# Two recurrences on one core: a lookup pair is moved from the large cell of the second recurrence to its small cell

## The chip, the cores and the metric

The kernel runs on one core of one Trainium2 chip. The metric is the device time of one execution in microseconds (us), shown as the median of three runs. Engines are named as in the profile: PE is TensorE's matmuls, PEld its weight loads, DVE is VectorE, ACT is ScalarE, POOL is GpSimd, SP is SyncE, which issues the DMAs.

## The reference

```python
B, LS, LN = 512, 64, 32
FM = [0, 0, 1, 1, 2, 2, 3, 3, 4, 5, 5]
...
        def step(carry, xt):
            h, c = carry
            g = xt @ Wx + h @ Wh + b
            i, f, gg, o = jnp.split(g, 4, axis=-1)
            c = jax.nn.sigmoid(f) * c + jax.nn.sigmoid(i) * jnp.tanh(gg)
            h = jax.nn.sigmoid(o) * jnp.tanh(c)
            return ((h, c), None)
...
m_from = lstm_last(base_emb[from_seq], seq_Wx, seq_Wh, seq_b)
m_to = lstm_last(base_emb[to_seq], seq_Wx, seq_Wh, seq_b)
...
        x = jnp.concatenate([ne[nums], fe[fr]], axis=-1)
        return lstm_last(x, Wx, Wh, b)
nwf = jax.vmap(enc)(nwf_num_emb[fm], nwf_freq_emb[fm], nwf_Wx[fm], nwf_Wh[fm], nwf_b[fm], nwf_numbers, nwf_freqs)
...
return jax.nn.relu(feats @ reduce_W + reduce_b)
```

The inputs have 2048 rows. There are two kinds of recurrence (LSTM). The first, `seq`, takes 64 steps with a state of 64 values over two token sequences that share their weights. The second, `nwf`, takes 32 steps with a state of 8 values for 11 features that use 6 sets of weights. Each of its steps looks up a number and a frequency in tables of 1000 rows. The last states and some single lookups go through one final matrix product.

## The kernel before

**Cells.** A step of a recurrence for one half of its data is a cell. `CELLS` sets one order of all cells, and every engine follows it. In a round r from 1 to 31 the order is: A and B, the two halves of `seq` step 2r; C, the large half of `nwf` step r-1 (features 0 to 7, 1024 columns); D and E, the two halves of `seq` step 2r+1; F, the small half of `nwf` step r-1 (features 8 to 10, 384 columns). The letters are used throughout. A round has six cells; round 0 has only its four `seq` cells, and a last round has only C and F.

**A cell** computes four gates on PE (`gate`, L515). Gates 0, 1 and 3 go through two PSUM buffers, `ab0` and `ab1`, used in turn; the forget gate has its own, `f_ps`. ACT applies the functions (`activate`, L555, L562, L564; `activate_f`) and releases the `ab` buffer. POOL multiplies gates 0 and 1 (`input_product`, `ig`, L585), DVE scales the old cell state (`scale_c`, L593) and adds (`add_c`, L598, at the start of the next cell), ACT takes the tanh (L555), POOL makes the new state (`new_h`, L612).

**Lookups** for `nwf` run beside the cells. The index of a table row is split into a low digit (0 to 127) and a high digit (0 to 7). Eleven pairs of lookups (0 to 10) belong to each round. For one pair, SP loads the low digits on all 128 partitions and the high digits (L416, L421); DVE compares (`compare_pair`, `hot`, L428); PE multiplies the one-hot matrix with the tables into `e_ps` (`look_up`, 24 matmuls, L438); DVE keeps the part that the high digit asks for (`keep_wanted`, `kept`, L450). There is one `e_ps`, so a look_up waits for the keep_wanted of the pair before it. A compare is made two pairs ahead of its look_up, into two `hot` buffers. Once both types of a feature set are kept, PE reduces them to that set's input (`set_input`, L465) in an `ab` buffer, and ACT copies it out (`store_x`, L478). Sets 0 to 3 and 5 take two pairs each, set 4 takes pair 8 alone.

**Where they stand.** `PAIRS_AT` gives each cell its pairs; `SETS_AT` gives the cell after a set's last pair that set's input. In a `seq` cell PE's order is gate 0, first look_up, set inputs, gate 1, second look_up, lookup of a later `seq` token (L401), forget gate, gate 3. In an `nwf` cell the set inputs and the first look_up stand ahead of gate 0:

```python
                    if CELLS[n][0] == "seq":
                        gate(pe, n, 0)
                        for p in pairs[:1]:
                            look_up(pe, p)
                        sum_sets(pe, n)
                    else:
                        sum_sets(pe, n)
                        for p in pairs[:1]:
                            look_up(pe, p)
                        gate(pe, n, 0)
                    gate(pe, n, 1)
                    for p in pairs[1:]:
                        look_up(pe, p)
```

The order of use of `ab0` and `ab1` is the list `USES`; `begin_use` makes PE wait until ACT has released the use two before. DVE's order in a cell is add_c of the cell before, first keep_wanted, compare of a `seq` token (L390), in F of rounds 1 to 29 the splitting of a later round's indices into digits (`make_digits`, L314 to L339), two compares, second keep_wanted, scale_c. POOL waits ahead of `input_product` until the compares of its cell are done. SP issues the loads of a pair four pairs ahead, each after the compare that frees its buffer.

Of the kernel before, what the change touches and what calls it, by code (L numbers as in the profile page):

```python
# [71 lines left out]
SETS_AT = [[] for _ in CELLS]  # L72
for _r in range(NWF_T):
    _j = NPAIRS * _r
    _share = [3, 3, 3, 2] if _r == 0 else [2, 2, 2, 2, 2, 1]
    _first = NUMBER["seq", 2 * _r, 0]
    for _k, _n in enumerate(_share):
        PAIRS_AT[_first + _k] = list(range(_j, _j + _n))
        _j += _n
        SETS_AT[_first + _k + 1] += [(_r, m) for m in range(NSETS)  # L80
                                     if _j - _n <= NPAIRS * _r + SET_LAST[m] < _j]
# [827 lines left out]
```

## Time and profile before

| | |
|---|---|
| median of 3 runs | 1803.08 us (1800.8 to 1803.32) |
| the profiled execution | 1799.57 us, its span 1797.7 us |
| mean granted clock of TensorE | 0.987 |
| PE busy | 93% of the span |
| DVE, ACT busy | 81% each |
| POOL busy | 53% |
| chain that ended last | PE 64%, ACT 18%, POOL 7%, issue 6%, DMA 1% |
| read from HBM | 474.17 MB, with the writes 267 GB/s |

The span runs from the first to the last instruction. The shares are means over a ramp of some 120 us, 31 rounds that look alike and a short end. "Idle" in a row is the time in which the row's engine had nothing to run just before it, with the instruction that ended the wait. A wait is told by its idle time or, since matmuls overlap, by the distance from one start to the next.

### The profile page before, as it was taken

To read this page: it belongs to the slowest core of one execution; us is meant where nothing else is said; L and a number is where in the kernel's file an instruction comes from. 1 tells how busy PE (TensorE), PEld (TensorE's weight loads), DVE (VectorE), ACT (ScalarE), POOL (GpSimd) and SP (SyncE) were. 2 spreads that over 40 slices of the span, in tenths; PEclk is the share of its full clock that TensorE was granted. 3 is DMA by queue.
4 is the path that set the end of the run, shared out by engine and by line. 5 is a ranking of instruction groups with operands and counts; after the bars stand their busy time and mean duration, and the time that the engine had idled before them with its cause. 6 is when DMAs were issued, how large, how long until landed. Compare 5 with 4: busy or idle time off the path is not lost.

```text
span 1797.7 us, 59515 instructions
## 1 busy us (share of the span) xinstructions
PE 1680.6 (93%) x24900; PEld 765.0 (43%) x24900; DVE 1462.9 (81%) x1443; ACT 1464.5 (81%) x2531; POOL 944.8 (53%) x478
## 2 busy tenths in 40 slices
PE   2789999999999999999999999999999999999995
PEld 0234444444444444444444444444444444444444
DVE  6768888888888888988888888888888888888771
ACT  1468888888888888888888888888888888888883
POOL 5346666666666666444444444444554444444552
PEclk9899999999999999999999999999999999999997
DMA  6868898999988988889898888989888888888832
GB/s 224 299 223 261 281 290 285 275 289 277 293 279 284 286 284 285 276 270 298 277 284 289 275 277 278 290 277 285 280 286 279 282 272 296 283 277 282 282 119 49
DMA packets 153476, 484.37 MB, mean 269 GB/s; under 512 B 39240, under 2 KB 95096, under 8 KB 108024
## 3 DMA queue, kind: packets, MB, share of 16 engines
q1 hardware_dynamic: 149532, 479.52, 82.5%
q8 instruction: 198, 3.24, 0.7%
q0 software_dynamic: 2560, 0.15, 0.5%
q10 hardware_dynamic: 1116, 0.88, 0.1%
q14 instruction: 70, 0.57, 0.1%
HBM read 474.17 MB, written 6.09 MB: 267 GB/s over the span
## 4 chain that ended last, share of the span: by engine, by line
PE 64%; ACT 18%; POOL 7%; issue 6%; DMA 1%; SPq 0%; DVE 0%; ACTq 0%; POOLq 0%
PE ab L515 28%; PE e_ps L438 15%; PE f_ps L515 10%; ACT gate L555 10%; PE ab L465 7%; POOL nwf_h L612 4%; ACT tanh_c L555 4%; POOL ig L585 4%; PE ab L401 3%; ACT seq_x L408 2%; ACT f_ps L564 1%; ACT gate L564 1%; ACT nwf_x L478 1%; DMA last_h<-nwf_h 0%; PE e_ps L828 0%
## 5 line engine op out<-in xcount | busy, mean ns | idle before, releaser
L585 POOL TENSOR_TENSOR ig<-gate 128x1024 f32<-128x1024 f32 x192 | 411.1, 2141 | 810.1 <-ACT seq_x L408 404.2
L428 DVE TENSOR_SCALAR hot<-low,cst 128x4096 bf16<-128x4096 bf16 x352 | 453.4, 1288 | 152.8 <-PE e_ps L438 149.4
L438 PE MATMUL e_ps<-hot,tab 128*32 128x512 bf16 x8448 | 527.2, 384 | 15.9 <-DVE kept L450 15.9
L450 DVE SCALAR_TENSOR_TENSOR kept<-high,cst,e_ps 128x1024 f32<-128x1024 uint8 x352 | 448.8, 1275 | 32.9 <-PE e_ps L438 22.1
L515 PE MATMUL ab<-seq_h,seq_wh 64*64 64x512 f32 x3072 | 411.0, 593 | 0.0
L438 PEld LDWEIGHTS e_ps<-hot,tab 128*32 128x32 bf16 x8448 | 204.3, 97 | 399.0 <-issue 228.9
L612 POOL TENSOR_TENSOR seq_h<-gate,tanh_c 128x1024 f32<-128x1024 f32 x128 | 303.9, 2374 | 1.4 <-ACT tanh_c L555 1.4
L562 ACT ACTIVATE gate<-ab 128x1024 f32<-128x1024 f32 x256 | 263.2, 1028 | 18.2 <-PE ab L515 15.0
L555 ACT ACTIVATE tanh_c<-seq_c 64x512 f32<-64x512 f32 (+1 forms) x384 | 241.9, 630 | 25.3 <-POOL nwf_h L612 22.2
L555 ACT ACTIVATE gate<-ab 64x512 f32<-64x512 f32 (+1 forms) x384 | 228.3, 595 | 11.5
L564 ACT ACTIVATE gate<-ab,nwf_bias 128x256 f32<-128x256 f32 (+1 forms) x384 | 147.4, 456 | 104.0 <-PE ab L515 99.9
L465 PE MATMUL ab<-kept,cst 128*32 128x256 f32 (+1 forms) x3072 | 189.5, 365 | 28.7 <-ACT gate L555 28.7
L515 PE MATMUL ab<-nwf_x,nwf_w 64*64 64x256 f32 (+1 forms) x2304 | 201.6, 366 | 7.2 <-ACT gate L555 5.5
L515 PE MATMUL ab<-nwf_h,nwf_w 64*64 64x256 f32 (+1 forms) x2304 | 204.9, 361 | 0.0
L408 ACT CAST seq_x<-ab 128x1024 bf16<-128x1024 f32 x128 | 129.6, 1013 | 69.7 <-PE ab L401 65.5
L593 DVE TENSOR_TENSOR f_ps<-seq_c,f_ps 128x1024 f32<-128x1024 f32 x128 | 157.3, 1229 | 28.8 <-ACT f_ps L562 16.7
L515 PE MATMUL ab<-seq_x,seq_wx 64*64 64x512 bf16 x1536 | 165.2, 385 | 10.0 <-issue 7.2
L598 DVE TENSOR_TENSOR seq_c<-ig,f_ps 128x1024 f32<-128x1024 f32 x128 | 156.3, 1221 | 8.3 <-POOL ig L585 3.3
L515 PEld LDWEIGHTS ab<-seq_h,seq_wh 64*64 64x64 f32 x3072 | 118.5, 133 | 89.4 <-issue 60.1
L562 ACT ACTIVATE f_ps<-f_ps 128x1024 f32<-128x1024 f32 x128 | 129.0, 1008 | 27.7 <-PE f_ps L515 27.7
L465 PEld LDWEIGHTS ab<-kept,cst 128*32 128x32 f32 x3072 | 88.3, 109 | 148.1 <-issue 59.0
L555 ACT ACTIVATE gate<-ab,nwf_bias 64x256 f32<-64x256 f32 (+2 forms) x288 | 125.4, 447 | 9.2 <-PE ab L515 5.9
(67 smaller groups left out, 1608.5 us busy)
## 6 DMA issues: line engine op xcount, KB each, us to landing
low<-low_digits SPq DMA_DIRECT2D x352, 1024.0 KB, 8.0
tok<-seq_tokens SPq DMA_DIRECT2D x128, 384.0 KB, 4.9
high<-high_digits SPq DMA_DIRECT2D x1408, 32.0 KB
raw<-in_indices SPq DMA_DIRECT2D x32, 176.0 KB
low_digits<-low_of SPq DMA_DIRECT2D x32, 88.0 KB, 3.0
high_digits<-high_of SPq DMA_DIRECT2D x32, 44.0 KB, 3.6
gate<-in_tokens SPq DMA_DIRECT2D x1, 1024.0 KB, 5.7
low<-last_h SPq DMA_DIRECT2D x11, 64.0 KB
```

Of the source, the lines that this page charges most:

```text
L408: nc.scalar.copy(seq_x[:, s % X_RING, :, :], ab[USE["sx", s] % 2][:, :, :]).then_inc(ab_done, 1)
L428: nc.vector.tensor_scalar(hot[:, p % HOT_RING, :, :, :].rearrange("p g u c -> p (g u c)"), low[:, p % LOW_RING, :, :].rearrange("p u c -> ...
L438: last = nc.tensor.matmul(e_ps[32 * g:32 * g + 32, i, :], tab[:, part, 2 * m + ty, :], hot[:, p % HOT_RING, g, i, :], start=(part == 0), s ...
L450: nc.vector.scalar_tensor_tensor(out=kept[:, p % KEPT_RING, :, :].rearrange("p u c -> p (u c)"), in0=high[:, p % HIGH_RING, :, :].rearrang ...
L465: last = nc.tensor.matmul(to[32 * q:32 * q + 32, 0, 0:n], cst[:, C_RED + 32 * ty:C_RED + 32 * ty + 32], kept[:, (NPAIRS * r + p) % KEPT_RI ...
L515: last = nc.tensor.matmul(flat(bank)[to:to + 64, cols], lhs(rows, half, block), rhs(rows, block, a, b), start=start, stop=stop)
L555: last = nc.scalar.activation(to[rows, a:a + c], of[there, a:a + c], function, bias=0.0 if bias is None else bias[there, :])
L562: return nc.scalar.activation(to, of, GATES[g][1])
L564: last = nc.scalar.activation(to[:, a:a + c], of[:, a:a + c], GATES[g][1], bias=bias)
L585: nc.gpsimd.tensor_tensor(ig[:, cols], gates[0][:, n % 2, cols], gates[1][:, n % 2, cols], ALU.mult).then_inc(ig_ready, 1)
L593: nc.vector.tensor_tensor(f, c_of(n), f, ALU.mult).then_inc(c_scaled, 1)
L612: nc.gpsimd.tensor_tensor(h_of(n), gates[3][:, n % 2, cols], tanh_c[:, cols], ALU.mult).then_inc(h_ready, 1)
```

## The change

One line of the table of pairs: in rounds 1 to 31 the large cell C gets one pair in place of two and the small cell F two in place of one. Cells D and E keep two pairs each, but of numbers one lower: D gets 5 and 6 (6 and 7 before), E gets 7 and 8 (8 and 9), F gets 9 and 10 (10). The places of the set inputs follow from this. Set 2 moves from D to E, set 3 from E to F, where it now stands ahead of set 4. Set 1 in C and set 5 in A stay.

```diff
-    _share = [3, 3, 3, 2] if _r == 0 else [2, 2, 2, 2, 2, 1]
+    _share = [3, 3, 3, 2] if _r == 0 else [2, 2, 1, 2, 2, 2]
```

On PE in C, before, from gate 1's last matmuls to the forget gate (`e_ps` is the second look_up):

```order
L515 MATMUL ab1<-nwf_h0,nwf_w 64x256 x4
L438 MATMUL e_ps<-hot,tab 32x512 x24
L515 MATMUL f_ps<-nwf_x,nwf_w 64x256 x4
L515 MATMUL f_ps<-nwf_h0,nwf_w 64x256 x4
L515 MATMUL f_ps<-nwf_x,nwf_w 64x256 x4
```

Behind it on PE in D, before, from gate 0 to the token lookup (`kept` is the input of set 2):

```order
L515 MATMUL ab1<-seq_x,seq_wx 64x512 x4
L515 MATMUL ab1<-seq_h,seq_wh 64x512 x4
L438 MATMUL e_ps<-hot,tab 32x512 x24
L465 MATMUL ab0<-kept,cst 32x256 x8
L515 MATMUL ab1<-seq_x,seq_wx 64x512 x4
L515 MATMUL ab1<-seq_h,seq_wh 64x512 x4
L438 MATMUL e_ps<-hot,tab 32x512 x24
L401 MATMUL ab0<-seq_hot,seq_tab 32x512 x8
```

The same piece of D with the change:

```order
L515 MATMUL ab1<-seq_x,seq_wx 64x512 x4
L515 MATMUL ab1<-seq_h,seq_wh 64x512 x4
L438 MATMUL e_ps<-hot,tab 32x512 x24
L515 MATMUL ab0<-seq_x,seq_wx 64x512 x4
L515 MATMUL ab0<-seq_h,seq_wh 64x512 x4
L438 MATMUL e_ps<-hot,tab 32x512 x24
L401 MATMUL ab1<-seq_hot,seq_tab 32x512 x8
```

The second look_up of C is gone, D has no set input, and D's gate 1 takes `ab0`, which C's gate 3 used last.

On PE from E's gate 3 into F, before (the `32x128` row is set 4's input):

```order
L515 MATMUL ab0<-seq_h,seq_wh 64x512 x4
L465 MATMUL ab1<-kept,cst 32x128 x8
L438 MATMUL e_ps<-hot,tab 32x512 x24
L515 MATMUL ab0<-nwf_x,nwf_w 64x256 x2
L515 MATMUL ab0<-nwf_x,nwf_w 64x128 x2
```

And with the change:

```order
L515 MATMUL ab1<-seq_h,seq_wh 64x512 x4
L465 MATMUL ab0<-kept,cst 32x256 x8
L465 MATMUL ab1<-kept,cst 32x128 x8
L438 MATMUL e_ps<-hot,tab 32x512 x24
L515 MATMUL ab0<-nwf_x,nwf_w 64x256 x2
L515 MATMUL ab0<-nwf_x,nwf_w 64x128 x2
```

Two set inputs stand in a row, and the second takes `ab1`, the buffer of E's gate 3. A second look_up stands later in F, between gate 1 and the forget gate.

On DVE in F and into A, before, from the splitting of digits to A's token compare:

```order
L339 CAST high_of<-wrap 128x352
L428 TENSOR_SCALAR hot<-low,cst 128x4096
L593 TENSOR_TENSOR f_ps<-nwf_c,f_ps 128x384
L598 TENSOR_TENSOR nwf_c<-ig,f_ps 128x384
L450 SCALAR_TENSOR_TENSOR kept<-high,cst,e_ps 128x1024
L390 TENSOR_SCALAR seq_hot<-tok,cst 96x2048
```

And with the change:

```order
L339 CAST high_of<-wrap 128x352
L428 TENSOR_SCALAR hot<-low,cst 128x4096 x2
L450 SCALAR_TENSOR_TENSOR kept<-high,cst,e_ps 128x1024
L593 TENSOR_TENSOR f_ps<-nwf_c,f_ps 128x384
L598 TENSOR_TENSOR nwf_c<-ig,f_ps 128x384
L450 SCALAR_TENSOR_TENSOR kept<-high,cst,e_ps 128x1024
L390 TENSOR_SCALAR seq_hot<-tok,cst 96x2048
```

A second compare and a second keep_wanted now stand between the digits and the state of F. On SP the token loads of D and E move ahead of one pair's loads each; POOL's order is the same.

## Rows read from the trace of the kernel before

**Rows 1.** The page, part 1: busy time of each engine, share of the span.
```profile
PE 1680.6 (93%) x24900; PEld 765.0 (43%) x24900; DVE 1462.9 (81%) x1443; ACT 1464.5 (81%) x2531; POOL 944.8 (53%) x478
```
**Rows 2.** Timeline of DVE, add_c of F in two rounds: start us, us, instruction.
```profile
1171.15 0.55 DVE L598 TENSOR_TENSOR nwf_c<-ig,f_ps 128x384 f32<-128x384 f32 x1
...
1224.04 0.56 DVE L598 TENSOR_TENSOR nwf_c<-ig,f_ps 128x384 f32<-128x384 f32 x1
```
**Rows 3.** Timeline of PE, C into D (last bracket: idle before, and releaser).
```profile
1192.76 1.48 PE L438 MATMUL e_ps<-hot,tab 128*32 128x512 bf16 x24
1194.17 0.66 PE L515 MATMUL f_ps<-nwf_x,nwf_w 64*64 64x256 f32 x8
...
1198.86 1.48 PE L438 MATMUL e_ps<-hot,tab 128*32 128x512 bf16 x24
1200.83 1.07 PE L465 MATMUL ab<-kept,cst 128*32 128x256 f32 x16 [0.50 <-ACT gate L555]
1201.83 0.41 PE L515 MATMUL ab<-seq_x,seq_wx 64*64 64x512 bf16 x4
...
1203.03 1.48 PE L438 MATMUL e_ps<-hot,tab 128*32 128x512 bf16 x24
1204.34 0.61 PE L401 MATMUL ab<-seq_hot,seq_tab 96*32 96x512 bf16 x8
```
**Rows 4.** Timeline of ACT in C: gate 1, forget gate, gate 3.
```profile
1192.90 1.57 ACT L564 ACTIVATE gate<-ab,nwf_bias 128x256 f32<-128x256 f32 x4 [0.16 <-PE ab L515]
...
1196.19 1.54 ACT L564 ACTIVATE f_ps<-f_ps,nwf_bias 128x256 f32<-128x256 f32 x4
1197.92 2.77 ACT L555 ACTIVATE gate<-ab,nwf_bias 128x256 f32<-128x256 f32 x6 [0.18 <-PE ab L515]
```
**Rows 5.** Timeline of PE, E through F into A.
```profile
1211.69 1.48 PE L438 MATMUL e_ps<-hot,tab 128*32 128x512 bf16 x24
1213.31 0.61 PE L401 MATMUL ab<-seq_hot,seq_tab 96*32 96x512 bf16 x8
...
1214.95 0.39 PE L515 MATMUL ab<-seq_x,seq_wx 64*64 64x512 bf16 x4
...
1216.12 0.65 PE L465 MATMUL ab<-kept,cst 128*32 128x128 f32 x16
1216.59 1.48 PE L438 MATMUL e_ps<-hot,tab 128*32 128x512 bf16 x24
1218.22 0.65 PE L515 MATMUL ab<-nwf_x,nwf_w 64*64 64x256 f32 x8 [0.16 <-ACT gate L555]
...
1222.90 1.48 PE L438 MATMUL e_ps<-hot,tab 128*32 128x512 bf16 x24
1224.75 1.07 PE L465 MATMUL ab<-kept,cst 128*32 128x256 f32 x16 [0.37 <-ACT gate L555]
```
**Rows 6.** Timeline of ACT, gate 3 of E.
```profile
1216.27 1.81 ACT L555 ACTIVATE gate<-ab 128x512 f32<-128x512 f32 x3
```
**Rows 7.** Timeline of DVE in F: keep_wanted, later the compare.
```profile
1218.64 1.27 DVE L450 SCALAR_TENSOR_TENSOR kept<-high,cst,e_ps 128x1024 f32<-128x1024 uint8 x1
...
1221.57 1.28 DVE L428 TENSOR_SCALAR hot<-low,cst 128x4096 bf16<-128x4096 bf16 x1
```
**Rows 8.** Timeline of DVE in A and B: the token compare in each.
```profile
1172.81 1.12 DVE L390 TENSOR_SCALAR seq_hot<-tok,cst 96x2048 bf16<-96x2048 bf16 x1
...
1182.03 0.75 DVE L390 TENSOR_SCALAR seq_hot<-tok,cst 96x2048 bf16<-96x2048 bf16 x1
```
**Rows 9.** Timeline of PE, two long waits outside the rounds.
```profile
64.10 2.33 PE L438 MATMUL e_ps<-hot,tab 128*32 128x512 bf16 x20 [2.75 <-DVE kept L450]
...
1753.73 1.07 PE L465 MATMUL ab<-kept,cst 128*32 128x256 f32 x16 [2.27 <-ACT gate L555]
```
**Rows 10.** Stretches: us; busy (count) of PE, PEld, DVE, ACT, POOL; PEclk; DMA share; GB/s.
```profile
63.70:67.10 3.40, 3.00 (x32) 1.27 (x32) 0.40 (x2) 0.00 (x0) 3.40 (x2) 0.50 0.77 274
1750.00:1756.00 6.00, 3.73 (x57) 2.25 (x54) 1.12 (x2) 4.47 (x10) 3.35 (x2) 1.00 0.02 4
```

## The prediction, made before the changed kernel was run

> **What bounds the kernel now.** The page's busy times come first: PE is busy for 93% of the span, DVE and ACT for 81% each [rows 1]. Such shares don't tell what a moved step costs, so the next view is the timeline of one round. The same add of F stands at 1171.15 and at 1224.04, so a round takes 52.89 us [rows 2], and 31 rounds with lookups make some 1640 of the 1797.7 us. In a round PE hardly rests. The reader is to see where its few waits stand and who ends them. In D, from the first look_up to set 2's input is 1.97 us, where a look_up that is followed without a wait has a slot of 1.31 (1203.03 to 1204.34); ACT's gate 3 of C ends that wait [rows 3]. In E the token lookup comes 1.62 after the look_up, 0.31 late. In A set 5's input comes 1.85 after the look_up, 0.54 late. In F gate 0 comes exactly 3.27 after gate 3 of E began (1214.95 to 1218.22) and is again released by ACT [rows 5]. So PE's work and the release of the two `ab` buffers by ACT bound the round together. ACT is the tight one in C: its gates there follow each other with idle times of 0.16 and 0.18 us [rows 4].
>
> **The change, part by part.** The number of matmuls, compares, keeps, copies and DMAs is the same. What counts is where PE's pieces meet a wait. Times below are those of the shown round, carried on as if the change began in its C.
>
> *C and D.* PE loses the second look_up of C, a slot of 1.41 us (1192.76 to 1194.17), and in D set 2's input, 1.00 us (1200.83 to 1201.83), with its wait of 0.66 [rows 3]. If all of that counted, D's gate 1 would come 3.07 us earlier. But D's gate 1 now needs the buffer of C's gate 3, which ACT releases. ACT's forget gate in C ends at 1197.73 and its gate 3 takes 2.77 [rows 4]; with PE earlier it loses only its idle 0.18 and ends at 1200.51. A release is followed by PE 0.14 us later (1200.69 to 1200.83), so D's gate 1 starts at 1200.65 instead of 1201.83: **1.18 us** gained. PE has then stood since its look_up, which now begins at 1197.45 and runs 1.48: a new wait of about 1.7 us (1.9 against its slot). DVE's and POOL's part of C gets shorter too, but the cell state of C needs ACT's forget gate, which hardly moves, so nothing is gained there.
>
> *E.* D still ends on the same pieces, and the 0.31 us that the token lookup waits in E falls away, because the set copy it needs comes as early as the rest; about 0.1 comes back where gate 1 waits for ACT's gate 0. Gate 3 of E begins 1.18 + 0.31 - 0.1 = **1.4 us** earlier.
>
> *F, first half.* Set 3's input stands 1.17 us after gate 3 of E, as set 4's did. Set 4's input now needs the buffer of E's gate 3. Before, it was F's gate 0 that needed it, and set 4's input and the look_up ran inside that wait: ACT's gate 3 takes 1.81 and ends 3.13 after PE's gate 3 began [rows 5, 6]. So set 4's input comes 3.27 after gate 3 of E, and behind it, in PE's order, stand the look_up and gate 0. Its own slot is 0.47 (1216.12 to 1216.59), the look_up's 1.41, so gate 0 comes 5.15 after gate 3 of E instead of 3.27: **1.88 us** lost. Set 3's input, 1.07 us long, lies inside the wait and leaves PE idle for about 1.0.
>
> *F, second half, and A.* The new look_up between gate 1 and the forget gate costs its slot of **1.41**. By PE alone A's look_up would then stand 7.95 (1214.95 to 1222.90) + 1.88 + 1.41 = 11.24 after gate 3 of E. It waits for the keep of pair 10, which DVE now makes at the end of F. The keep of pair 9 starts when its look_up is done, 3.27 + 0.47 + 1.48 = 5.22 after gate 3 of E; from a keep to the first compare is 2.93 with the digits between them [rows 7]; each compare moves DVE on by 1.2 and the keep ends 1.27 after it starts. That is 5.22 + 2.93 + 1.2 + 1.2 + 1.27 = 11.82, and A's look_up starts about 0.1 later, at 11.9: **0.6 us** of new wait. A's old wait of 0.54 for ACT falls away, since ACT has had the time.
>
> *Sum.* -1.4 + 1.88 + 1.41 + 0.6 - 0.54 = **+1.95, say 2.0 us a round**. In the rest of A and in B everything is shifted alike, so the round repeats with this. Twenty-nine rounds have digits in F; without them the last two have no wait for the keep of pair 10 and, at the end, some of the cost falls into the wait of 2.27 us in front of the last C [rows 9]. 29 x 2.0 + about 2 = 60 us.
>
> *What I cost at nothing.* The token loads on SP that move ahead of one pair's loads, and those loads: a pair is loaded four ahead, which is more than a cell, and the longer round gives them more time. If they came late, a compare would wait for a DMA. POOL's product in F now waits for the second compare of F; what it feeds, the cell state and tanh of F, is wanted on PE only a round later. Cover gone, it would delay ACT in A. POOL and DVE together are the unknown: the token compare takes 1.12 us in A, with POOL at work, and 0.75 in B [rows 8]. In the new stretch of F the digits and compares should find POOL at rest. The bounds for that stretch are no wait at all (0.6 less) and 0.37 more, the difference of those two rows, for each of F's two compares (0.75 more). I take neither: the row of B, without POOL, is the nearer one, and the durations in the sum are of that kind.
>
> A pause of PE of this length is where its clock comes in. In the ramp a wait of 2.75 us ended at 64.10, and the granted clock of the 3.4 us from 63.70 was 0.50, which is 1.2 of 2.4 GHz; near the end PE waited 2.27 us up to 1753.73, and the clock stayed at 1.00 [rows 9, 10]. The new waits of 1.7, 1.0 and 0.6 are all shorter than that, so the sum has no term for it. The Trainium skill ("TensorE: Matmul & The Clock Gate", Part 1: The HAM clock gate) says that the throttled rate is the default state and that activity releases it; this speaks against any change that makes PE pause. The row at 64.10 agrees with it, and no row here shows a fall after a pause as short as the new ones. By the rows the sum is +60; by the rule, were these pauses enough, it is that of the second rival below.
>
> The sum is made against the profiled execution, 1799.57 us, and gives 1859.6. The median of the runs is 3.5 us above that execution, so for the median I say **1863 us**, 3.3% slower.
>
> **The rivals.**
>
> 1. *DVE is not late* (chance 0.10). The keep of pair 10 comes in time and 0.6 a round falls away: 1.4 x 31 = 43, 1846 us. For it: it rests on five DVE steps in a row, each rounded. Against: there is no wait among them that could shrink.
>
> 2. *The clock falls* in D's new wait (0.05). A fall costs half of 3.4 us, 1.7 a round: 3.7 x 31 = 115, 1918 us. For it: the clock did fall after a pause of 2.75. Against it: it did not after one of 2.27, and the forecast's longest is 1.7 [rows 9, 10].
>
> 3. *Faster: ACT follows PE* (0.03). If ACT in C and E is late only because PE feeds it late, then with PE ahead both releases come earlier, and D's 1.9 and set 4's 1.2 beyond its slot in F vanish: 2.0 - 3.1 = -1.1 a round, -34, 1769 us. It turns from slower to faster once ACT's gate 3 of C ends about 1.2 us before 1200.51. Against it: in C there are only 0.16 and 0.18 of idle time between ACT's gates [rows 4], so it can't move by 1.2.
>
> 4. *Nothing moves* (0.02): the 1.41 of C and the 1.41 of F cancel, and the other waits too; 1803 us. That the change doesn't do what it says can be left out: the order of instructions shows pair 5 behind D's gate 0 and two look_ups in F.
>
> **How the numbers follow.** The forecast has 0.75, rival 1 0.10, the others 0.10 together; 0.05 is left for a slower outcome of another size. The range takes in rival 1 and the bounds of the DVE stretch: at the low end 0.6 a round less and another 0.2 of rounding, 1.2 x 31 = 37, 1840; at the high end 2.75 x 31 = 85, 1888. It leaves out rivals 2 to 4 and the rest of the unlikely. Measurements of this kernel can tell about 0.2%, 3.6 us, from no change. Faster by more 0.03, within it 0.02, slower by more 0.95.
>
> **What would show it.** In the profile after: rounds of 54.9 us; in D, PE's gate 1 about 3.2 us after the look_up, released by ACT's gate 3 (L555), a wait of some 1.7; in F, two L465 in a row with about 1 us of idle time between them, released by the same line; in A, the look_up waiting some 0.6 for DVE's keep (L450); the wait of A's set input gone; the clock at 1.00 through all rounds. Wrong would be a gate 1 of D that starts right after its look_up, a second L465 in F without a wait, or a granted clock below 1 between 120 and 1750 us.

## The result, and the profile after

| | before | after |
|---|---|---|
| median (runs) | 1803.2 us (1800.8 to 1805.72, 4) | 1863.38 us (1861.24 to 1864.23, 4) |
| ratio, 95% interval | | 1.0332 [1.0314, 1.035] |
| span of the profiled execution | 1797.7 us | 1862.4 us (execution 1864.23) |
| round without a stall of PE | 52.89 us | 55.12 us |

The kernel became 60 us slower. The changed kernel's page gives the busy times, the granted clock by slices, and the chain that ended last:

```profile
PE 1680.3 (90%) x24900; PEld 759.7 (41%) x24900; DVE 1446.3 (78%) x1443; ACT 1459.9 (78%) x2531; POOL 929.1 (50%) x478
...
PEclk9899999999999999999999999999999999999997
...
PE 49%; DVE 17%; ACT 13%; POOL 8%; issue 7%; DMA 1%; DVEq 0%; SPq 0%; POOLq 0%; ACTq 0%
```

PE is busy for the same 1680 us as in [rows 1], in a span that is 65 us longer: the change added no work, it added waits. In the chain PE's share fell from 64% to 49%, and DVE's, 17%, is new. The same add of F as in [rows 2], timeline of DVE, in two rounds of the changed kernel:

```profile
1213.20 0.55 DVE L598 TENSOR_TENSOR nwf_c<-ig,f_ps 128x384 f32<-128x384 f32 x1
...
1268.33 0.55 DVE L598 TENSOR_TENSOR nwf_c<-ig,f_ps 128x384 f32<-128x384 f32 x1
```

A round takes 55.13 us here, 2.24 more than before. PE's waits, from the list of waits (us in total, times, longest):

```profile
PE ab L515 <- ACT gate L555: 50.0, 31, 1.8
PE ab L465 <- ACT gate L555: 32.7, 32, 1.0
PE e_ps L438 <- DVE kept L450: 31.6, 30, 8.9
```

There are three per round: D's gate 1, the second set input of F, the first look_up of A. The sums hold the ramp and the end too: the wait of 8.9 us in the third row lies in the ramp. The three stand in the timeline of PE as follows. C into D (answers to [rows 3]):

```profile
1229.99 1.48 PE L438 MATMUL e_ps<-hot,tab 128*32 128x512 bf16 x24
1231.40 0.66 PE L515 MATMUL ab<-nwf_x,nwf_w 64*64 64x256 f32 x8
...
1239.54 1.48 PE L438 MATMUL e_ps<-hot,tab 128*32 128x512 bf16 x24
1242.77 0.41 PE L515 MATMUL ab<-seq_x,seq_wx 64*64 64x512 bf16 x4 [1.75 <-ACT gate L555]
```

E through F into A (answers to [rows 5]):

```profile
1252.63 1.48 PE L438 MATMUL e_ps<-hot,tab 128*32 128x512 bf16 x24
1254.26 0.62 PE L401 MATMUL ab<-seq_hot,seq_tab 96*32 96x512 bf16 x8 [0.15 <-ACT nwf_x L478]
...
1255.91 0.39 PE L515 MATMUL ab<-seq_x,seq_wx 64*64 64x512 bf16 x4
...
1257.08 1.07 PE L465 MATMUL ab<-kept,cst 128*32 128x256 f32 x16
1259.18 0.65 PE L465 MATMUL ab<-kept,cst 128*32 128x128 f32 x16 [1.03 <-ACT gate L555]
1259.61 1.50 PE L438 MATMUL e_ps<-hot,tab 128*32 128x512 bf16 x24
1261.05 0.65 PE L515 MATMUL ab<-nwf_x,nwf_w 64*64 64x256 f32 x8
...
1262.92 1.48 PE L438 MATMUL e_ps<-hot,tab 128*32 128x512 bf16 x24
...
1267.97 1.48 PE L438 MATMUL e_ps<-hot,tab 128*32 128x512 bf16 x24 [0.62 <-DVE kept L450]
1269.26 1.05 PE L465 MATMUL ab<-kept,cst 128*32 128x256 f32 x16
```

Behind each wait stands its releaser. Timeline of ACT: forget gate and gate 3 of C ([rows 4]), tanh of D's state and a set copy in E, gate 3 of E ([rows 6]):

```profile
1238.43 1.50 ACT L564 ACTIVATE f_ps<-f_ps,nwf_bias 128x256 f32<-128x256 f32 x4
1239.95 2.77 ACT L555 ACTIVATE gate<-ab,nwf_bias 128x256 f32<-128x256 f32 x6
...
1251.80 1.92 ACT L555 ACTIVATE tanh_c<-seq_c 128x512 f32<-128x512 f32 x3 [0.59 <-POOL nwf_h L612]
1253.75 0.37 ACT L478 COPY nwf_x<-ab 128x256 f32<-128x256 f32 x1
...
1257.23 1.81 ACT L555 ACTIVATE gate<-ab 128x512 f32<-128x512 f32 x3
```

Timeline of DVE in F ([rows 7]): keep of pair 9, the two compares behind the digits, keep of pair 10.

```profile
1261.22 1.28 DVE L450 SCALAR_TENSOR_TENSOR kept<-high,cst,e_ps 128x1024 f32<-128x1024 uint8 x1 [1.53 <-PE e_ps L438]
...
1264.15 2.48 DVE L428 TENSOR_SCALAR hot<-low,cst 128x4096 bf16<-128x4096 bf16 x2
1266.55 1.28 DVE L450 SCALAR_TENSOR_TENSOR kept<-high,cst,e_ps 128x1024 f32<-128x1024 uint8 x1
```

ACT's gate 3 of C ends at 1242.72, and PE's gate 1 of D follows at 1242.77. ACT's gate 3 of E ends at 1259.04, and set 4's input follows at 1259.18. DVE's keep of pair 10 ends at 1267.83, and A's look_up follows at 1267.97.

### The profile page after: what moved, and what is told of

Its sections match the earlier page's. It is cut to its first block, busy times and chain, and to the rows that moved or that the text cites. A ratio compares the mean times of both kernels' runs of the same rounds, so it can differ in the third digit from the quotient of the medians.

```text
span 1862.4 us, 59515 instructions
## 1 busy us (share of the span) xinstructions
PE 1680.3 (90%) x24900; PEld 759.7 (41%) x24900; DVE 1446.3 (78%) x1443; ACT 1459.9 (78%) x2531; POOL 929.1 (50%) x478
## 3 DMA queue, kind: packets, MB, share of 16 engines
q8 instruction: 198, 3.24, 0.7%
## 4 chain that ended last, share of the span: by engine, by line
PE 49%; DVE 17%; ACT 13%; POOL 8%; issue 7%; DMA 1%; DVEq 0%; SPq 0%; POOLq 0%; ACTq 0%
PE ab L515 19%; PE e_ps L438 15%; PE f_ps L515 6%; DVE hot L428 6%; PE ab L465 6%; DVE kept L450 5%; ACT tanh_c L555 4%; POOL nwf_h L612 4%; POOL ig L585 4%; ACT gate L555 3%; ACT f_ps L564 3%; PE ab L401 3%; ACT gate L564 2%; DVE f_ps L593 2%; DVE seq_hot L390 1%
## 5 line engine op out<-in xcount | busy, mean ns | idle before, releaser
L438 PE MATMUL e_ps<-hot,tab 128*32 128x512 bf16 x8448 | 528.2, 384 | 31.7 <-DVE kept L450 31.6
L450 DVE SCALAR_TENSOR_TENSOR kept<-high,cst,e_ps 128x1024 f32<-128x1024 uint8 x352 | 449.1, 1276 | 94.4 <-PE e_ps L438 81.8
L428 DVE TENSOR_SCALAR hot<-low,cst 128x4096 bf16<-128x4096 bf16 x352 | 448.7, 1282 | 37.4 <-PE e_ps L438 31.6
L438 PEld LDWEIGHTS e_ps<-hot,tab 128*32 128x32 bf16 x8448 | 210.8, 97 | 410.1 <-issue 260.1
L555 ACT ACTIVATE tanh_c<-seq_c 64x512 f32<-64x512 f32 (+1 forms) x384 | 241.8, 630 | 22.7 <-POOL nwf_h L612 19.6
L564 ACT ACTIVATE gate<-ab,nwf_bias 128x256 f32<-128x256 f32 (+1 forms) x384 | 147.4, 456 | 137.7 <-PE ab L515 132.3
L555 ACT ACTIVATE gate<-ab 64x512 f32<-64x512 f32 (+1 forms) x384 | 228.4, 595 | 9.5
L465 PE MATMUL ab<-kept,cst 128*32 128x256 f32 (+1 forms) x3072 | 188.8, 364 | 32.7 <-ACT gate L555 32.7
L593 DVE TENSOR_TENSOR f_ps<-nwf_c,f_ps 128x1024 f32<-128x1024 f32 x64 | 57.1, 892 | 196.8 <-ACT f_ps L564 196.8
L465 PEld LDWEIGHTS ab<-kept,cst 128*32 128x32 f32 x3072 | 88.7, 109 | 145.4 <-issue 49.9
```

The source lines that it names most:

```text
L428: nc.vector.tensor_scalar(hot[:, p % HOT_RING, :, :, :].rearrange("p g u c -> p (g u c)"), low[:, p % LOW_RING, :, :].rearrange("p u c -> ...
L438: last = nc.tensor.matmul(e_ps[32 * g:32 * g + 32, i, :], tab[:, part, 2 * m + ty, :], hot[:, p % HOT_RING, g, i, :], start=(part == 0), s ...
L450: nc.vector.scalar_tensor_tensor(out=kept[:, p % KEPT_RING, :, :].rearrange("p u c -> p (u c)"), in0=high[:, p % HIGH_RING, :, :].rearrang ...
L465: last = nc.tensor.matmul(to[32 * q:32 * q + 32, 0, 0:n], cst[:, C_RED + 32 * ty:C_RED + 32 * ty + 32], kept[:, (NPAIRS * r + p) % KEPT_RI ...
L555: last = nc.scalar.activation(to[rows, a:a + c], of[there, a:a + c], function, bias=0.0 if bias is None else bias[there, :])
L564: last = nc.scalar.activation(to[:, a:a + c], of[:, a:a + c], GATES[g][1], bias=bias)
```

## The experiments

Times are medians; a ratio is to the kernel before, measured on the same chip (medians there 1801.5 to 1802.7 us). "Round" is a round without a stall of PE; the last part tells what those stalls are. Where a kernel has one line more, L438, L450, L465 and L555 appear as L439, L451, L466 and L556.

### The first half of F: a look_up between the two set inputs

Changed kernel, order of PE in C and F:

```diff
-                        sum_sets(pe, n)
+                        for r, m in SETS_AT[n][:1]:
+                            set_input(pe, r, m)
                         for p in pairs[:1]:
                             look_up(pe, p)
+                        for r, m in SETS_AT[n][1:]:
+                            set_input(pe, r, m)
```

> The changed kernel, with F's first look_up between its two set inputs instead of behind both. My theory: set 4's input waits 1.0 us for the buffer of E's gate 3, and the look_up behind it could have run in that time. F's gate 0 then comes 3.96 us after gate 3 of E instead of 5.14; DVE's keep of pair 9 starts about 1.5 earlier, so A's look_up comes at 10.5 instead of 12.06 after gate 3 of E: 1.56 x 31 = 48 us less, 1815. Rival, the loss in F is the moved PE work itself and no wait: within 5 us of 1863.

Measured: 1814.62 us, ratio 1.007 [1.0054, 1.0087]; round 53.50. PE's timeline, set 4's input in F and A's look_up:

```profile
1227.63 0.62 PE L465 MATMUL ab<-kept,cst 128*32 128x128 f32 x16
...
1234.70 1.48 PE L438 MATMUL e_ps<-hot,tab 128*32 128x512 bf16 x24 [0.23 <-DVE kept L450]
```

The look_up runs inside the time in which ACT finishes gate 3 of E, and the wait of 1.03 is gone. Keep 9 starts earlier with its look_up, so A's wait shrinks from 0.62 to 0.23 as well. No work was removed, and 49 of the 60 us came back. So most of the net loss is an order in which two set inputs stand next to each other and the second needs a buffer that is not yet free.

### The second half of F: who sets the start of A

Changed kernel, the digits made in C:

```diff
-ROUND_AT = {(2 if _r == 2 else NUMBER["nwf", _r - 3, 1]): _r
+ROUND_AT = {(2 if _r == 2 else NUMBER["nwf", _r - 3, 0]): _r
...
```

> The changed kernel, with the splitting of digits moved from F to C of the same round, where DVE stands idle for 5.9 us. My theory: in F the digits lie on DVE's chain to the keep of pair 10, for which A's look_up waits 0.62 us a round. Without them in F the keep comes 1.7 us earlier and PE alone sets that look_up: 0.6 x 29 = 18 us less, 1845. Rival, DVE is not what A waits for: 1863, unchanged.

Measured: 1846.44 us, ratio 1.0247 [1.0228, 1.0266]; round 54.42, that is 0.70 less. A's look_up has no wait any more, while D's 1.74 and F's 1.03 stay:

```profile
1193.34 0.64 PE L465 MATMUL ab<-kept,cst 128*32 128x128 f32 x16 [1.03 <-ACT gate L555]
...
1201.44 1.48 PE L438 MATMUL e_ps<-hot,tab 128*32 128x512 bf16 x24
```

Changed kernel, F's second look_up (pair 10) cut to 8 of its 24 matmuls:

```diff
+                parts = 1 if p % NPAIRS == 10 and p >= NPAIRS else 3
-                for part in range(3):
+                for part in range(parts):
```

> The changed kernel, with F's second look_up (pair 10) doing 8 of its 24 matmuls, the second and third part of the table values left out for that pair. 0.85 us of PE is taken from F each round. My theory: A's look_up waits for DVE's keep of pair 10, whose chain starts at the look_up of pair 9 and does not wait for that of pair 10, so the wait only gets longer: 1863, unchanged within 3 us. Rival, the second look_up costs its PE time: 0.85 x 31 = 26 us less, 1837.

Measured: 1862.53 us, ratio 1.0341 [1.032, 1.0361]; round 55.13. What PE saves in F it waits in A:

```profile
1212.47 1.48 PE L439 MATMUL e_ps<-hot,tab 128*32 128x512 bf16 x24 [1.49 <-DVE kept L451]
```

The wait grew from 0.62 to 1.49, by the 0.87 that the look_up lost. In the changed kernel the end of F belongs to DVE's row of keep, digits, two compares and keep, and no longer to PE.

### C and D: what a look_up in C is worth

Kernel before, C's second look_up (pair 5) cut in the same way to 8 of 24 matmuls:

```diff
+                parts = 1 if p % NPAIRS == 5 and p >= NPAIRS else 3
-                for part in range(3):
+                for part in range(parts):
```

> The kernel before, with C's second look_up (pair 5) doing 8 of its 24 matmuls: the second and third part of the table values are left out for that pair. 0.85 us of PE is taken from C each round. My theory: behind C, D waits for ACT's gate 3 of C, which can come only 0.2 us earlier, so the gain is 0.2 x 31 = 6 us, 1797. Rival, PE bounds C and its work counts in full: 0.85 x 31 = 26 us, 1777.

Measured: 1792.02 us, ratio 0.9948 [0.993, 0.9966]. The cut took 27 us of PE's work (31 rounds of 0.87) and the time fell by 10. Over the rounds, the median from C's second look_up to D's first fell from 6.10 to 5.23, all of the 0.87; from there to D's second look_up it rose from 4.17 to 4.81, so D gave 0.64 back. Set 2's input in D, which waited 0.50 in [rows 3]:

```profile
1033.96 1.07 PE L466 MATMUL ab<-kept,cst 128*32 128x256 f32 x16 [1.13 <-ACT gate L556]
```

The rest, 0.23 a round, is 7 of the 10 us. The forecast of 1797 was 5 us too high, and the rival's 1777 is further off: three quarters of a look_up's work in C go into the wait for ACT.

The next edit takes the same place from the other side. ACT's gate 3 of C is written as whole-width instructions instead of two halves that change places. It was tried once in the changed kernel, once in the kernel before (`whole` marks the gates that keep their old form; C's gate 3 is the one that gets the new one):

```diff
-            last = at_h(to, of, pieces(n, g), GATES[g][1]) if g == 3 else in_place(to, of, n, g)
+            whole = g == 3 and CELLS[n][0] == "seq" or g == 3 and CELLS[n][2] == 1
+            last = at_h(to, of, pieces(n, g), GATES[g][1]) if whole else in_place(to, of, n, g)
```

> The changed kernel, with ACT's gate 3 of C done as whole-width instructions like gates 0 and 1 (the exchange of the two halves of the second feature block is left out), 1.57 us instead of 2.77. D's gate 1 is then released 1.2 us earlier. My theory: behind it D's second look_up needs the keep of pair 5, which DVE makes after the add of C, and that comes no earlier; so only 0.3 of the 1.2 counts: 9 us less, 1854. Rival, ACT's gate 3 alone sets D: 1.2 x 31 = 37 us less, 1826.

Measured: 1856.21 us, ratio 1.0292 [1.0272, 1.0313]; round 54.94. PE in D:

```profile
1236.75 0.41 PE L515 MATMUL ab<-seq_x,seq_wx 64*64 64x512 bf16 x4 [0.55 <-ACT gate L564]
...
1238.96 1.48 PE L438 MATMUL e_ps<-hot,tab 128*32 128x512 bf16 x24 [0.94 <-DVE kept L450]
```

The wait for ACT fell from 1.75 to 0.55, and 0.94 of the 1.20 came back two rows later as a wait for DVE, whose keep stands behind the new cell state of C. So ACT's gate 3 held D up, and DVE's keep is the next to do so, only 0.2 us earlier.

> The kernel before with ScalarE's gate 3 of C as whole-width instructions (the exchange of halves is left out, so part of the new state of C is not computed as in the reference). In the kernel before, set 2's input in D waits for this gate, with PE idle for 0.66 us. In the changed kernel the same edit took 7 us (from 1863.4 to 1856.2), 0.25 us a round. Theory, D's release is the only thing that the gate 3 of C holds up: if the edit shortens ScalarE's gate 3 by as much as it did there, the release comes 0.2 to 0.7 us earlier, 6 to 20 us less, 1782 to 1796. Rival, ScalarE is late in C before gate 3 and the gate's form does not matter: 1800 to 1803.

Measured: 1778.38 us, ratio 0.9867 [0.9852, 0.9882]; round 52.19, which is 0.70 less. D runs without any wait:

```profile
1186.36 1.48 PE L438 MATMUL e_ps<-hot,tab 128*32 128x512 bf16 x24
1187.67 1.04 PE L465 MATMUL ab<-kept,cst 128*32 128x256 f32 x16
```

The gain of 23 us is beyond the forecast's end of 20: the wait of 0.66 went whole in all 31 rounds (31 x 0.70 = 22). The rival falls. Here no wait for DVE takes its place.

### Put together

The changed kernel with both orders, digits in C and look_up between the set inputs:

> The changed kernel with both edits: the look_up between F's set inputs, and the digits in C. With the look_up moved, A still waits 0.22 us for DVE's keep; without the digits in F that goes too. My theory: 0.25 to 0.45 us a round less than with the look_up alone, 1802 to 1807, so that the whole loss in F is undone and only the gain of C and D set against the moved look_up is left: about the kernel before. Rival, another wait takes their place: 1815 or more.

Measured: 1810.83 us, ratio 1.0042 [1.0027, 1.0056]: a miss. The round is 53.19, 0.3 below that of the look_up between the set inputs, as expected. But PE stood more often with no releaser that the profile names: over 29 rounds the mean is 53.60 with the look_up alone, 0.10 above a round without a stall, and 53.52 with both, 0.33 above. The "issue" row of PE's waits, first with the look_up between the set inputs alone, then with both:

```profile
PE ab L515 <- issue: 11.4, 7, 3.6
```

```profile
PE ab L515 <- issue: 21.3, 18, 3.6
```

Not all of these are stalls. Three in each row (8.9 us) lie in the ramp and the end, and one of the 7 (1.9 us) and five of the 18 (6.2 us) are D's gate 1, which starts 0.05 us after ACT's gate has ended, as in the rows with a named releaser. What is left went from 3 (0.6 us) to 10 (6.3 us).

Both kernels still lose 1.74 in D. ACT in C stands in order gate 0, gate 1, tanh of B's state, forget gate, gate 3, and before gate 0 it idles (1.99 us in the changed kernel, `ACT L564 gate`, while PE works on C's first matmuls). So ACT's tanh of the cell before was moved ahead of gate 0 in C and F, with a second `tanh_c` buffer. First in the kernel before:

```diff
+                        tanh_of(act, n - 1)
                     activate(act, n, 0)
...
                     activate(act, n, 1)
-                    if not is_seq:
-                        tanh_of(act, n - 1)
```

> The kernel before with the same edit of ACT's tanh and its second buffer alone. My theory: C with two look_ups is bound by PE at gate 3, so D gains nothing; E's 0.3 and A's 0.5 us of wait go: 0.8 x 31 = 25 us less, 1778. It tells how much of the edit's worth needs the pairs moved. Rival, the edit is worth the same in both: 1750.

Measured: 1790.36 us, ratio 0.994 [0.992, 0.996]; round 52.66, only 0.23 less, and 12 us in all where 25 were forecast. PE in D and F:

```profile
1194.81 1.07 PE L465 MATMUL ab<-kept,cst 128*32 128x256 f32 x16 [0.49 <-ACT gate L555]
...
1215.14 0.65 PE L515 MATMUL ab<-nwf_x,nwf_w 64*64 64x256 f32 x8 [0.46 <-ACT gate L564]
```

D's wait stays at 0.49: in C ACT now waits 1.73 us for PE's forget gate, which stands behind the second look_up, so here ACT follows PE. E's and A's waits did go: the token lookup of E comes 1.30 after the look_up (1.62 before), set 5's input in A 1.30 after its look_up (1.85 before). But F's gate 3 got a wait of 0.46 for ACT's gate 0 of F, which now stands behind the tanh, and the way from F's gate 0 to A's look_up grew from 4.68 to 5.35. Then in the changed kernel with both orders:

> The third edit on top of both: in C and F ACT takes the tanh of the cell before ahead of gate 0 instead of behind gate 1, with a second tanh buffer so that it need not wait for POOL. ACT idles 2 us ahead of gate 0 in both cells. My theory: C's forget gate and gate 3 on ACT come 1.4 us earlier, the add of C with them, so D's wait of 1.75 shrinks to 0.35; E's token lookup no longer waits 0.3 for POOL. 1.7 x 31 = 53 us less than both edits, 1752, faster than the kernel before by 2.8%. Rival, PE or DVE takes the wait's place in D: no better than 1790.

Measured: 1771.08 us, ratio 0.9833 [0.9808, 0.9857]. The round is 51.52, 1.67 below that with both orders (1.7 forecast), and D's wait fell from 1.74 to 0.40. The time is 19 us above the forecast: the mean of its 29 rounds is 52.14, 0.62 above a round without a stall. The last kernel has the same, with the digits back in F:

> The changed kernel with F's first look_up put between its two set inputs (as in lookup_between, 1814.6 us) and, in the large and small cells, ScalarE's tanh of the previous cell put ahead of gate 0 (as in both_tanh, 1771.1 us), but with pair digits made in F as the change has them. It tells apart where the irregular rounds of both_tanh come from, in which PE is late in C and F without a wait that the profile shows. Forecast for an undisturbed round: both_tanh's 51.5 us, or up to 0.25 more, since the keep of pair 10 gets the wait of A's look_up back (0.22 in lookup_between). Theory 1, the digits in C bring the irregular rounds: here they are as few as in lookup_between (mean round 0.1 over an undisturbed one), mean 51.6 to 51.9, about 1755 to 1763 us. Theory 2, they come wherever PE runs without a wait, digits or not: mean round 0.6 over an undisturbed one as in both_tanh, 52.1 to 52.4, about 1771 to 1778 us.

Measured: 1763.43 us, ratio 0.9789 [0.9776, 0.9803], faster than both kernels. The round is 51.83 and the mean of 29 is 52.02. A's look_up and D's gate 1:

```profile
1200.35 1.48 PE L438 MATMUL e_ps<-hot,tab 128*32 128x512 bf16 x24 [0.24 <-DVE kept L450]
...
1228.94 0.41 PE L515 MATMUL ab<-seq_x,seq_wx 64*64 64x512 bf16 x4 [0.40 <-ACT gate L555]
```

Its round is 0.31 longer than with the digits in C, and yet it is some 8 us faster; the excess of the mean over a round without a stall is 0.19 us instead of 0.62. Theory 1 (the digits in C bring the stalls) had the excess at 0.1 and 1755 to 1763 us, theory 2 at 0.6 and 1771 to 1778: neither holds it, the first is nearer. The excess is that of one profiled execution of each kernel, and those two have nearly the same span (1765.8 us here, 1764.6 with the digits in C), so it carries less than the medians. Why the digits on DVE should matter to PE's stalls no run shows.

## Why the prediction was right

The forecast was 1863 us and the median came at 1863.38. Term by term, from the distances on PE in the shown round (before to after):

| stretch | predicted | measured |
|---|---|---|
| C's first set input to D's gate 1 | -1.18 | 14.98 to 13.66, -1.32 |
| D's gate 1 to E's gate 3 | -0.21 | 13.12 to 13.14, +0.02 |
| E's gate 3 to F's gate 0 | +1.88 | 3.27 to 5.14, +1.87 |
| F's gate 0 to A's look_up | +1.41 + 0.6 | 4.68 to 6.92, +2.24 |
| A's look_up to A's gate 1 | -0.54 | 2.85 to 2.27, -0.58 |
| sum | +1.95 | +2.24 (with 0.01 elsewhere) |

*D* was right in its mechanism: two slots of PE's work, 2.41 us, left the path, and of the 3.07 of work and wait 1.32 came back as time. PE's new wait of 1.75 (predicted 1.7) ends with ACT's gate 3 of C. The whole-width gate 3 moved it in both kernels; the two cuts show that a look_up's work counts for a quarter in C of the kernel before and for nothing in F of the changed one, where another engine sets the next release. The 0.14 that the term fell short is ACT's gate 3, 0.23 earlier instead of 0.18, and PE's start 0.05 after it (1242.72 to 1242.77) instead of 0.14.

*E* is the step that failed. I wrote that the 0.31 us of the token lookup would fall away "because the set copy it needs comes as early as the rest". It came 1.63 after the look_up, as before (1.62 in [rows 5]). The copy did come as early as the rest, and just that keeps the wait: from C's set input to the copy is 1.30 less than before, and to D's gate 1 1.32 less. To take the wait away, the copy had to gain 0.31 more than PE. What ties the two together, before, in timelines of DVE, POOL and ACT (second compare of D, new state of C, the copy):

```profile
1204.64 1.29 DVE L428 TENSOR_SCALAR hot<-low,cst 128x4096 bf16<-128x4096 bf16 x1 [1.06 <-PE e_ps L438]
...
1208.38 2.38 POOL L612 TENSOR_TENSOR nwf_h<-gate,tanh_c 128x1024 f32<-128x1024 f32 x1
...
1212.79 0.37 ACT L478 COPY nwf_x<-ab 128x256 f32<-128x256 f32 x1
```

And with the change, in timelines of DVE and POOL (both compares of D, product of D, new state of C):

```profile
1244.22 2.64 DVE L428 TENSOR_SCALAR hot<-low,cst 128x4096 bf16<-128x4096 bf16 x2
...
1247.00 2.37 POOL L585 TENSOR_TENSOR ig<-gate 128x1024 f32<-128x1024 f32 x1 [5.46 <-DVE hot L428]
1249.33 2.38 POOL L612 TENSOR_TENSOR nwf_h<-gate,tanh_c 128x1024 f32<-128x1024 f32 x1
```

The copy at 1253.75 stands on ACT behind the tanh of D, and that waits for POOL's new state of C. On POOL that state stands behind the product of D, which waits for DVE's second compare of D, and this compare needs the `hot` buffer that PE's second look_up of D frees. That look_up ends at 1204.51 before and at 1245.45 with the change, and the copy starts 8.28 and 8.30 later. So the copy follows PE's own work in D and moves with it. The tanh moved in the kernel before shows the link: with the second `tanh_c` buffer the tanh of D no longer waits for POOL, and E's wait is gone (1.30 from look_up to token lookup).

*F's first half* was right to 0.01 us, the wait being 1.03 (predicted about 1.0). Putting the look_up between the two set inputs took away that wait.

*F's second half and A*: the mechanism was right, the sum 0.23 short. From E's gate 3 to A's look_up it took 12.06 instead of 11.9: keep 9 started 5.31 after that gate (5.22 predicted), the keep to the first compare took 2.93 and the two compares 2.40 as predicted, and PE followed the keep after 0.14 instead of 0.1. Also 11.9 less 11.24 is 0.66, which the text rounded to 0.6. The row with POOL at rest was the right one to take for the compares: 2.40 for two. The loads, costed at nothing, cost nothing more: compares wait 3.3 us in all for low digits, in the kernel before as in the changed one.

The total was closer than its parts, and that is luck. 0.29 a round too little is 8 us over 29 rounds. Against it stand the rounds with a stall of PE: over 29 rounds the mean is 53.06 in the kernel before, 0.17 above a round without one, and 55.16 in the changed kernel, 0.03 above. So the mean round grew by 2.10 us, 61 in 29 rounds, where I had 58; the sum has no term for stalls. The last rounds and the end took 3.4 us more, where I had about 2. The profiled span grew by 64.7, and the medians, 1803.2 and 1863.38, lie 60 apart.

*The rivals.* DVE was late by 0.62 (rival 1 falls; the digits in C and the cut in F show the wait each in its way). The clock did not fall (rival 2). The stretches hold the pauses of D and F (columns as in [rows 10]):

```profile
1241.00:1243.00 2.00, 0.25 (x8) 0.17 (x8) 1.97 (x3) 1.94 (x5) 0.54 (x1) 1.00 0.04 16
...
1256.00:1260.00 4.00, 2.97 (x56) 1.37 (x52) 3.16 (x3) 3.28 (x6) 4.00 (x2) 1.00 1.00 316
```

PE does little in the first, and the granted clock is 1.00, the level of 2.4 GHz, as it is in each of the eight stretches into which the time from 200 to 1750 us of the changed kernel was divided. The Trainium skill ("TensorE: Matmul & The Clock Gate", Part 1: The HAM clock gate) has the throttled rate as the default that activity releases; no run here shows a pause of 1.75 us that made it come back. ACT did not follow PE (rival 3): counted from C's set input its gate 3 of C ended after 13.61 instead of 13.84, only 0.23 earlier, though PE brought its work 1.4 earlier. Nor did the terms cancel (rival 4).

## What to carry to other kernels

When work is moved between stages, look for the wait on either side first: a piece that leaves a stage whose end another engine sets is worth little, and a piece that arrives in a stage can cost more than its own time if the pieces around it now need a buffer one step earlier or if it lengthens the row of another engine: from E's gate 3 to A's look_up the way grew by 4.11 us for a look_up of 1.41. Where two short pieces that use the same ring of buffers come to stand next to each other, put a long piece that needs no buffer between them; here that alone gave back 49 of 60 us. A wait goes only if what is waited for gains more than the engine that waits; "it comes as early as the rest" leaves the wait as it is. So a term of a sum that drops a wait needs the chain behind it, followed back over the engines: here it led back to PE itself.

## What the runs showed of the hardware that was not expected

Some rounds are longer by 0.3 to 2.7 us with no wait that the profile names: PE pauses, most often inside the gates of C or F. In the kernel before there are three pauses of 0.92 to 1.12 us, six rounds apart. One of them, timeline of PE in C:

```profile
1087.75 0.38 PE L515 MATMUL f_ps<-nwf_x,nwf_w 64*64 64x256 f32 x1
1089.25 0.44 PE L515 MATMUL f_ps<-nwf_x,nwf_w 64*64 64x256 f32 x4 [1.12 <-issue]
```

The trace has transfers of kind "instruction" on queue q8: 198 in the execution, 3.24 MB, so 16 KB each. PE's 49800 matmuls and weight loads and the 868 instructions of its sequencer, 50668 in all, are 256 a transfer. The two kernels with a look_up cut short have 49676 and 194 transfers, again 256 each: this is PE's own program. The queues of the DMA in the 8.9 us ahead of the pause, then up to its end:

```profile
q1 hardware_dynamic: 707, 2.53, 101.5%
```

```profile
q1 hardware_dynamic: 266, 0.90, 104.3%
q8 instruction: 1, 0.02, 2.6%
```

What PE did in the first of these stretches (columns as in [rows 10]):

```profile
1077.60:1086.50 8.90, 8.90 (x148) 4.43 (x144) 6.71 (x6) 6.43 (x13) 4.70 (x2) 1.00 1.01 284
```

PE ran 148 matmuls and 144 weight loads, more than the 256 of a transfer, and no transfer of its program came in this time, in which q1 kept the DMA engines full. That the load held it back is not shown: the 8.9 us at the same place a round earlier were as full (102.1%) and had one at their end. The next transfer began at 1086.58 and took 1.17 us, and 1.5 us after it landed PE went on.

The place of the pauses in PE's program tells more. In all twelve traces, between the ramp and the last round, PE has 65 waits of over 0.3 us that the profile puts down to "issue". Counted through the trace in blocks of 256 instructions of PE, 52 of them end at number 193 or 194 of a block, whatever the cell and the gate, and each of these ends 2.37 to 2.77 us after a transfer on q8 began, while the transfers come 3.5 to 17.3 us apart. The other 13 stand at other numbers and are no stalls: they end 0.05 to 0.15 us after a gate of ACT, like D's waits with a named releaser. In the kernel before, the transfers ahead of the three pauses began when PE was 412 to 414 instructions past a multiple of 256, the others between 200 and 1700 us at 163 to 368. So a pause comes where a transfer comes late against PE's place in its program. A round has 1579 instructions of PE, 6 transfers and 43 instructions over; six rounds make 258 of these, which brings the same phase back every sixth round.

The Trainium skill ("Runtime: NRT & Kernel Launch", Instruction fetch mechanics) says that instructions come in blocks of 16 KiB, 256 of them, by a DMA queue of the sequencer, and that the cost of crossing such a boundary is mostly hidden. The size agrees; in these rounds the crossing was not hidden.

In the changed kernel such a pause in C or F cost nothing: the three rounds that hold them take 55.11 to 55.13 us like the others, since PE waits for ACT in D and for DVE in A anyway. In the kernels that lost these waits the pauses came on top: with both orders and the early tanh 29 rounds take 18 us more than rounds without a stall would, and by the distances from start to start some 12 of these (an estimate) stand at the pauses. That PE waits there for its instructions is read from the place in the program and the times of the transfers. No run changed the supply, so what makes a transfer late, and why some kernels have more such pauses, stays open.
